# Selective scan on one core: filler products on TensorE, moved step-size and summing products, late coefficients on GpSimd

## The reference, cut to what matters

```
xn = (x - mu) * lax.rsqrt(var + eps) * ln_w + ln_b
x_in, z = split(xn @ W_in)                  # 256 channels each
xc = silu(causal_conv4(x_in) + conv_b)
dt_r, Bm, Cm = split(xc @ W_xproj)          # 8 + 16 + 16 columns
dt = softplus(dt_r @ W_dt + b_dt)
h  = h * exp(dt * A) + dt * B * xc          # step by step over 512 positions, 16 states
y  = sum_n h[n] * C[n] + xc * D_param
out = x + (y * silu(z)) @ W_out
```

## Time and profile before

| | us |
|---|---|
| median of 3 runs | 3111.35 (3110.55 to 3114.8) |
| profiled execution, its own time | 3111.72 |
| its span | 3110.0 |
| scan stage in it (first scan to last weighing) | 906.0 to 1350.7 |
| its mean granted clock | 0.954 |

### The profile page before, as it was taken

The page is one execution under the profiler, slowest core; times in us unless marked ns, Lnnn a source line. Parts: engine busy times, 40 slices in busy tenths (PEclk is TensorE's granted clock), DMA queues, the critical chain, the costliest instruction groups (busy, mean ns, idle before and its releaser), DMA issues. The chain is left out here.

```text
span 3110.0 us, 44512 instructions
## 1 busy us (share of the span) xinstructions
PE 2814.7 (91%) x14327; PEld 1760.4 (57%) x14354; DVE 1643.1 (53%) x4042; ACT 1511.5 (49%) x3086; POOL 1591.5 (51%) x1622
## 2 busy tenths in 40 slices
PE   6796997896778899767989999999999999999999
PEld 4564996775733344337974444444444444777776
DVE  4436444755368999974335555555555555211112
ACT  3431332332667877622235666666666664433333
POOL 0011775423768999933434555555555554699100
PEclk9898998887999999988989999999999999999999
DMA  5001667101122222243000000000000000000000
GB/s 174 0 24 56 206 206 188 43 1 40 49 82 70 79 75 82 74 122 116 22 12 1 1 0 0 0 0 0 0 0 0 0 1 13 16 8 8 14 7 28
DMA packets 91000, 141.36 MB, mean 45 GB/s; under 512 B 12315, under 2 KB 48038, under 8 KB 90838
## 3 DMA queue, kind: packets, MB, share of 16 engines
q1 hardware_dynamic: 76502, 116.83, 12.1%
q0 software_dynamic: 9728, 19.94, 2.6%
q10 hardware_dynamic: 4608, 2.56, 0.3%
HBM read 122.71 MB, written 24.97 MB: 47 GB/s over the span
## 5 line engine op out<-in xcount | busy, mean ns | idle before, releaser
L1790 POOL TENSOR_TENSOR l3a_p<-l3a_p,l3a_rden 128x512 f32<-128x512 f32 x512 | 521.5, 1040 | 482.2 <-DVE l3a_rden L1826 479.5
L1816 DVE CUSTOM_DVE_ANT_0 l3a_p<-bank,relative_bias 128x512 f32<-128x512 f32 x512 | 333.4, 689 | 211.2 <-PE bank L1965 204.4
L1886 ACT ACTIVATE l3a_p<-l3a_p,l3a_low 128x512 f32<-128x512 f32 x512 | 365.4, 719 | 4.5 <-DVE l3a_low L1816 4.5
L1974 PEld LDWEIGHTS bank<-ident,l3a_p 128*128 128x128 f32 x2048 | 228.5, 141 | 162.5 <-issue 157.9
L2731 POOL TENSOR_TENSOR l2a_dBu<-l2a_du,l2a_bs 128x1024 f32<-128x1024 f32 x128 | 299.1, 2351 | 32.9 <-DVE l2a_h L2974 30.6
L1892 ACT COPY l3a_pT<-bank 128x512 f32<-128x512 f32 x256 | 150.2, 587 | 324.2 <-PE bank L1974 323.8
L2974 DVE TENSOR_TENSOR_SCAN l2a_h<-bank,l2a_dBu 128x1024 f32<-128x1024 f32 x128 | 290.5, 2280 | 9.5 <-ACT bank L2873 8.3
L1559 ACT ACTIVATE l3f_h<-bank,l3f_b 128x512 f32<-128x512 f32 x256 | 175.5, 687 | 244.4 <-PE bank L1667 241.1
L1965 PE MATMUL bank<-l3a_kT,l3a_qT 64*128 64x512 f32 x1024 | 291.3, 645 | 1.2 <-ACT l3a_kT L1877 0.7
L1974 PE MATMUL bank<-ident,l3a_p 128*128 128x128 f32 x2048 | 273.6, 277 | 0.6 <-ACT l3a_pT L1892 0.5
L1676 PEld LDWEIGHTS bank<-l3f_w,l3f_h 128*128 128x128 f32 x2048 | 237.7, 192 | 27.2 <-issue 27.2
(11 more groups left out here) (523 smaller groups left out, 5008.0 us busy)
## 6 DMA issues: line engine op xcount, KB each, us to landing
l2a_bs<-l2a_b_rows SPq DMA_DIRECT2D x128, 256.0 KB, 3.3
l0fe_wi<-in_L_ffn_in_dram SPq DMA_DIRECT2D x40, 516.0 KB, 4.9
l0fe_wo<-in_L_ffn_out_dram SPq DMA_DIRECT2D x40, 320.0 KB, 3.3
by_place<-by_distance SPq DMA_DIRECT2D x16, 512.0 KB, 14.5
relative_bias<-by_place SPq DMA_DIRECT2D x16, 448.0 KB, 11.5
l3f_w<-in_L_ffn_W_dram SPq DMA_DIRECT2D x16, 256.0 KB, 3.1
switch_out<-in_L_ffn_out_dram SPq DMA_DIRECT2D x1, 2560.0 KB, 19.2
switch_in<-in_L_ffn_in_dram SPq DMA_DIRECT2D x1, 2064.0 KB, 14.4
```

Of the source, the lines that this page charges most:

```text
L1790: ins = pool.tensor_tensor(a, a, rden[:, t, h:h + 1].to_broadcast([P, S]), ALU.mult)
L1816: bk.drain(dve.tensor_tensor_reduce(p[u % 2][h][:, t, :], ps(job)[:], bias[:, u % HP * 2 + h, b0:b0 + S], 1.0, 3.0e38, ALU.add, ALU.min, l ...
L1886: ins = act.activation(a, a, ACT.Exp, bias=low[h][:, t:t + 1], scale=-1.0, accum_out=den[:, t, h:h + 1])
L1974: ins = pe.transpose(ps(job)[:, t * P:(t + 1) * P], p[u % 2][h][:, t, kt * P:(kt + 1) * P], chip.ident[:])
```

## The change

Six edits, all in `selective_scan`:

1. `keep_running(6)` instead of 5 at the start, and from round 1 on `keep_running(2, chip.psum[7])` at n = 0: two full products (four PE instructions) into bank 7 that nothing reads, after ACT has read the job before out of that bank.
2. The second `step_sizes` product moves from n = 2 to n = 3 (in round 0 from 4 to 5); it stands now behind the `spread` of its step.
3. The sum of POOL's tile of n = 0 moves from step 5 to step 6.
4. `keep_normed` for rows 0 and 1 moves from steps 10 and 15 to 8 and 11.
5. `rows_of(2)` in round 0 moves from n = 2 to n = 4.
6. Of `gains(2)` DVE keeps only the reciprocal; the three small operations that follow are POOL's, after its third `dBu`.

```diff
-        SHARED, LATER, ADDED_AT = (0, 3, 6), 4, {0: 5, 3: 12, 6: 13}
+        SHARED, LATER, ADDED_AT = (0, 3, 6), 4, {0: 6, 3: 12, 6: 13}
...
+                def late_gains():
+                    cut = slice(*PARTS[2])
+                    pool.wait_ge(inverted, 1)
+                    c.link(pool.tensor_tensor(shifts[:, :, cut], inv[:, :, cut], bcast(mv[:, cut, 0], n_before=2), ALU.mult))
+                    chip.apart(pool)
+                    pool.tensor_scalar(shifts[:, :, cut], shifts[:, :, cut], -1.0, 0.0, ALU.mult, ALU.add).then_inc(inv_ready, 1)
+                    pool.tensor_scalar(own_gain[:, cut], inv[:, 0, cut], 1.0, 0.0, ALU.add, ALU.add).then_inc(gains_ready, 1)
...
+                    if m == 2:
+                        late_gains()
...
-                    if m in (10, 15):
-                        keep_normed((10, 15).index(m))
+                    if m in (8, 11):
+                        keep_normed((8, 11).index(m))
...
-                        if n == 2:
+                        if n == 2 + late:
                             rows_of(q + 2)
...
-                gains(2)
+                cut = slice(*PARTS[2])
+                dve.wait_ge(std_ready, 3)
+                dve.reciprocal(inv[:, :, cut], std[:, :, cut]).then_inc(inverted, 1)
                 recur(0)
...
-                keep_running(5, c_bank)
+                keep_running(6, c_bank)
...
+                    if n == 0 and q:
+                        bk.wait_read(pe, ("bc", q + 1) if q + 1 < B else ("z", q - 1, 1), 0)
+                        keep_running(2, chip.psum[7])
                     if n == 1:
                         through(q)
+                    if n == 3 + late and q + 1 < B:
+                        step_sizes(q + 1, 1)
...
-                    if n in (1 + late, 2 + late) and q + 1 < B:
-                        step_sizes(q + 1, n - 1 - late)
+                    if n == 1 + late and q + 1 < B:
+                        step_sizes(q + 1, 0)
```

More of the change, by code:

```diff
@@ L2662, in selective_scan @@
         dve_order, cleared = sem("dve_order"), sem("bc_cleared")
+        inverted = sem("inverted")
         added, dtr_ready, pool_order = sem("answers_added"), sem("dtr_ready"), sem("pool_order")
```

## The result

| | before | changed |
|---|---|---|
| median | 3112.59 us (5 runs, 3110.55 to 3115.48) | 3098.2 us (5 runs, 3089.96 to 3099.79) |
| span of the profiled execution | 3110.0 us | 3096.4 us |
| ratio of the times, 95% | | 0.9949, 0.9933 to 0.9964 |

The changed kernel is faster by 0.5%, some 14 us. The forecast said 3093 us, range 3086 to 3103.

What follows compares the result with a forecast made beforehand. DVE was taken as the bound, busy 51.91 of a 55 us round, with POOL next at 51.00. Rounds 1 to 6 give -13.9 us and the start -4.0, together -17.9 off 3111.35: 3093 us, range 3086 to 3103.

Steps and rivals of the forecast that it cites:

- the 2.38 us wait: Round 2, DVE before weighing n = 4: idle 2.38 us for PE's spread; the PE edits were to remove it.
- a second fall: PE behind the second step-size product: clock falls again, slowing the sum of n = 4 and `give_out`, 1.2 us each.
- I expect it in about half of the rounds: Rounds 1 to 6: the clock falls behind the second step-size product in about half, 3 x 1.2 = 3.6 us back.
- and stays: Round's end: DVE's 0.39 us wait for ACT, a loop of DVE and ACT, was to remain.
- 0.5 at n = 11: End of PE's gapless string: the spread of n = 11 becomes 0.5 us late, so a round gains 2.2 us.
- It takes away the 0.33 at n = 7 and leaves the 0.5: Moving the n = 0 sum to step 6 removes DVE's 0.33 us wait but keeps 0.5 at n = 11.
- rounds 2 to 5 follow each other by 52.5 to 53.7: Sign in the changed profile: rounds 2 to 5 spaced 52.5 to 53.7 us instead of 54.7.
- (b): Rival: fillers too short, clock still falls at `through`; the order alone gains 9.6 us, giving 3102; chance 0.18.
- The start: Stage start and round 0: the edits on DVE, POOL and ACT save 4.0 us, bounds 1.5 and 5.
- (a): Rival: clock never falls in these rounds; gain 22.5 us, giving 3089 or a little less; chance 0.13.
- (c): Rival: POOL's queue takes DVE's place, rounds stay at 54; gain 5 us, 3106; chance 0.07.
- (d): Rival: later sum of POOL's n = 0 tile stalls POOL and delays `dBu`; +6.5 us, 3118; chance 0.04.

Runs made afterwards that it cites:

- experiment 4: Kernel before plus only the two filler products at n = 0 from round 1 on; ratio to before 0.9961.
- experiment 6: Changed kernel with the second step-size product back at n = 2, ahead of the spread of n = 4; ratio to before 0.9950.
- experiment 10: Changed kernel with POOL's tile of n = 0 summed at step 5 again instead of 6; ratio to before 0.9953.
- experiment 3: Changed kernel without the two filler products at n = 0, the sixth `keep_running` at the start kept; ratio to before 0.9983.
- experiment 5: Kernel before plus only the start edits (sixth `keep_running`, earlier `keep_normed`, later `rows_of(2)`, late `gains(2)` operations on POOL); ratio to before 0.9967.
- experiment 7: Changed kernel with all of `gains(2)` on DVE again, none of it on POOL; ratio to before 0.9961.
- experiment 9: The changed kernel run once more without edits, on the chip of the other experiments' kind; ratio to before 0.9942, median 3167.9 us.
- experiment 2: Changed kernel with POOL's tile of n = 0 summed at step 3, in PE's gap behind the second step-size product; ratio to before 0.9927.
- experiment 12: Changed kernel with POOL's tile of n = 0 summed at step 3 and five `keep_running` at the start; ratio to before 0.9919, median 3158.6 us.
- experiment 1: Changed kernel with step-size products over 128 rows, zero but for the first 8, same result; ratio to before 0.9931.
- experiment 8: Changed kernel with POOL's n = 0 sum at step 3, five `keep_running`, and `keep_normed` of row 0 behind the split's middle part; ratio to before 0.9918.
- experiment 11: Changed kernel with POOL's n = 0 sum at step 3 and the second step-size product back at n = 2; ratio to before 0.9909.

## Why the prediction was right, and where it was not

**Right in its mechanism at the head of the round.** The fillers keep the clock up, `through` takes 1.99 us (predicted 1.9), the spread of n = 4 is in time, the 2.38 us wait is gone. The step-size product stands at the place named for a second fall, and the fall comes there. Its price is that of the text: 54.42 - 53.24 = 1.18 us between rounds of the same kernel, in the changed kernel and in experiments 4, 6 and 10 alike; predicted 1.2.

**Its frequency was wrong.** "I expect it in about half of the rounds" rested on two rounds of before, one with it. It came in four of five, and five of five the second time. The rows of before misled: where the clock falls at `through`, the fall behind the transposes came in 3 of 15 rounds (rounds 1 to 5 of before and of experiments 3 and 5), and where `through` was at full clock in 22 of 29 (changed 4 of 5, experiments 4, 6, 7, 9, 10: 2 of 4, 3, 5, 5 and 3 of 5). These are not chances, and one fall doesn't prevent the other: a slow `through` makes the stretch come some 1.4 us later or more, mostly where rounds pass, and the fillers pulled it to where they fall. The prediction's "half" took each round for a draw of its own; whole traces fall or pass by where the first round happens to lie and by the round's length. Two falls more than expected in rounds 2 to 5: 2 x 1.2 = 2.4 us.

**The string behind it was mis-sized.** The text let each round keep 0.39 us for ACT "and stays", 0.5 at n = 11, and come to 54.7 - 2.2 = 52.5. A round without the fall takes 53.24, 0.74 longer. Its waits come to 1.37 us (0.21 + 0.75 for ACT, 0.23 at the spread, 0.18 at `give_out`) where the text had 0.89; the other 0.26 isn't accounted for. The step that failed is that the loop of DVE and ACT is closed: ACT's copy of the gate waits 0.91 us for PE, and with the sum of n = 0 taken out of PE's string (experiment 2) 0.24 of that wait is left and nothing of DVE's. The lateness also stood elsewhere than named: n = 11 late by 0.5 to 1.7 was the sign, and it was late by 0.23, while `give_out` was by 1.05 to 1.37 where the clock fell. "It takes away the 0.33 at n = 7 and leaves the 0.5" was right in kind: at step 5 DVE waits 0.98 at n = 7 and 0.38 for ACT, at step 6 it waits 0.23, 0.21 and 0.76. Four rounds at 0.74: 3.0 us.

These two make the miss. Rounds 2 to 5 were to gain 4 x 2.2 - 2 x 1.2 = 6.4 us and gained 1.1; 2.4 + 3.0 = 5.4 accounts for the 5.3. Rounds 1 and 6 gained 9.2, 1.7 more than the 7.5 left for them in the sum (20.0 - 4 x 2.71 = 9.2, minus 0.5 and one fall of 1.2): no fall came there. That is luck as far as round 1 goes: in experiments 6, 7 and 9 it fell. The sign "rounds 2 to 5 follow each other by 52.5 to 53.7" was not met, at 54.4, and the total came into the range since the range reached up to (b).

**The start was right in its sum**, -4.0 us of 4.0, and -3.8 alone (experiment 5), against a single trace of before; experiment 4, which has the start of before, took 75.6 in round 0. DVE's waits for POOL's `dBu` rose from 0.8 us to 8.1 as those for ACT went, so POOL's queue paced round 0, as the text had it. The late coefficients took 1.0 us on POOL with their waits (predicted 0.8), the cast waited 1.51 (1.3), the scan at the round's end 0.47 instead of 2.01. The sixth `keep_running` cost nothing that could be told (experiments 9 and 12).

**Edit 2** was to take away 2.38 us "right behind the sum of n = 2". It does bring the spread in time, but undone it costs nothing (experiment 6), since of that wait the fillers alone leave 0.82, and later waits take those up.

**The rivals.** (a), no fall at all, is what experiments 1 and 2 produce; there it is worth 6.1 us, 1.4 of it from the shorter rounds of experiment 1, and 10.3 with the sum in the gap. (b) was the case without fillers. (c) did not come: rounds of 52.15 us leave POOL busy 50.95 and DVE 51.70, so DVE is still the bound. (d)'s mechanism is there and small: POOL's product waited 0.93 us for the sum of its tile in round 3, and no `dBu` after round 0 was late for DVE.

**The Trainium skill.** The rule weighed in the prediction (TensorE: Matmul & The Clock Gate, section "Why this matters for your kernels": keep TensorE free of long idle gaps between bursts) would have seen no fall here, since the gaps left are 1.45 us and less. The trace disagrees: 0.50 granted behind such a gap. The same section says of products with few rows that one takes as long as a full one; 1.09 and 1.10 us agree. What experiment 1 adds is that the clock tells them apart. That the transposes weigh little for the clock, as the prediction read the row at 986, is not decided: they stand in experiments 1 and 2 too, where it didn't fall.

## What to carry to other kernels

When idle time of TensorE is filled to hold its clock, look for the next stretch of thin work behind it: here the fall moved 10 us down the round and gave back 1.2 us each time. Don't take one round's luck for the kernel's: a small shift of the stretch or of the round's length can turn falls on or off, so compare several rounds of more than one trace. Fill gaps with work that is due anyway before adding products that nothing reads; one sum moved into a gap of 1.45 us gained 10 us, as much as the whole PE part of the change. And test each edit with the others in place and alone: two of the six here were worth nothing together with the rest, and one of these gained 2.5 us once the gap was filled.

## What the runs showed of the hardware

- The granted clock fell to 0.50 behind two step-size products of 8 rows with 0.22 us ahead of the second and 1.45 behind it, in four and five of five rounds of the changed kernel; with the same instructions over 128 rows (experiment 1) in none, two of them at places where all 8-row rounds fell. The length of the instruction is the same.
- The same stretch can pass: in round 1 of the changed kernel and in two of five rounds of experiment 10 the transposes and the sum behind the same gap took 0.63 and 1.88 us, as at full clock. What decides it is where the stretch comes against instants that the program doesn't set: falls 54.61 us apart in rounds of 54.4 and of 54.7 us alike, and 45 rounds that separate by that place into 25 with the fall and 20 without. Filling the gap ends it (0 of 20 in experiments 2, 8, 11 and 12, at least six of them at places of the 25).
- A DVE operation on 24 columns beside POOL's products took 2.14 and 2.33 us, and 0.17 for the same shape in between (experiment 7). POOL's products of 2.35 us ran without a break there. That DVE had to wait for one of them to end is argued from the lengths, not shown.
- On POOL the three operations on 24 and 48 columns took 0.23 to 0.32 us each.
